# Transposed keys copied once into a compact buffer and placed in the padded operand by two DMAs, with the scores issued behind the next query projection

## The reference, cut to what matters

```python
        qkv = x @ Wqkv
        q, k, v = jnp.split(qkv, 3, -1)
        q = l2norm(q) * qs
        k = l2norm(k) * ksc
        q = q * cos * scale + rotate_half(q) * sin * scale
        k = k * cos * inv + rotate_half(k) * sin * inv
        ...
            sim = jnp.einsum('bhwie,bhwje->bhwij', bq, bk2) * QK_SCALE
            attn = jax.nn.softmax(sim, -1)
            out = jnp.einsum('bhwij,bhwje->bhwie', attn, bv2)
        ...
        return out @ Wo
```

## Time and profile before

| | us |
|---|---|
| median of 3 runs | 3313.89 |
| lowest, highest | 3313.37, 3315.62 |
| profiled execution, its own time | 3315.39 |
| span of the profiled execution | 3313.5 |

### The profile page before, as it was taken

One profiled execution on the slowest core, in us unless ns is written; L12 is line 12 of the kernel. 1 busy time (PEld: TensorE's weight loads), 2 busy tenths in 40 slices (PEclk: granted clock), 3 DMA queues, 4 the chain that ended last, 5 costly groups with the idle time before them and its releaser, 6 DMA issues. The chain is left out here.

```text
span 3313.5 us, 78774 instructions
## 1 busy us (share of the span) xinstructions
PE 3069.6 (93%) x28844; PEld 2169.1 (65%) x28844; DVE 2496.2 (75%) x3265; ACT 2434.9 (73%) x3708; POOL 2060.2 (62%) x1410
## 2 busy tenths in 40 slices
PE   8288886899999999999999999999999999999996
PEld 6276675666666676666666666666666666666662
DVE  3788886777778777787777777777777777777772
ACT  3366664687877787878787787878787877787872
POOL 0356554766666666666667666667666666666660
PEclk9689897999999999999999999999999999999997
DMA  1000001100001100001000011000110000100002
GB/s 45 13 23 22 19 22 45 37 20 19 19 19 26 45 19 19 19 19 53 19 19 19 16 26 45 19 19 19 27 45 19 19 19 17 32 21 19 20 19 58
DMA packets 80509, 84.53 MB, mean 26 GB/s; under 512 B 23734, under 2 KB 53908, under 8 KB 79668
## 3 DMA queue, kind: packets, MB, share of 16 engines
q1 hardware_dynamic: 79988, 82.40, 9.3%
q0 software_dynamic: 448, 1.20, 0.1%
HBM read 22.72 MB, written 2.10 MB: 7 GB/s over the span
## 5 line engine op out<-in xcount | busy, mean ns | idle before, releaser
L1325 POOL TENSOR_TENSOR qk_r<-qk_r,qk_t 128x1024 f32<-128x1024 f32 x384 | 915.6, 2385 | 669.0 <-DVE qk_r L1181 438.8
L807 PE MATMUL pa<-w_hi,xs_hi 128*128 128x512 f32 x1152 | 583.6, 507 | 68.6 <-DVE w_lo L1261 38.4
L1174 DVE TENSOR_REDUCE ss<-sq 128x16 f32<-128x1024 f32 x384 | 464.0, 1208 | 63.1 <-ACT sq L983 63.1
L1036 ACT COPY kT<-px 64x1024 f32<-64x1024 f32 x384 | 385.0, 1003 | 119.2 <-PE px L835 114.5
L1181 DVE TENSOR_TENSOR qk_r<-pa,rot 128x1024 f32<-128x1024 f32 x384 | 465.9, 1213 | 0.0
L1190 DVE TENSOR_TENSOR qk_t<-pa,rot 128x1024 f32<-128x1024 f32 x384 | 465.7, 1213 | 0.0
L807 PE MATMUL pa<-w_hi,xs_lo 128*128 128x512 f32 x1152 | 458.1, 398 | 0.0
L807 PE MATMUL pa<-w_lo,xs_hi 128*128 128x512 f32 x1152 | 457.4, 397 | 0.0
L835 PEld LDWEIGHTS px<-ident_sb,qk_r 128*128 128x128 f32 x3072 | 361.4, 142 | 113.3 <-issue 74.9
L1334 POOL TENSOR_TENSOR qk_r<-qk_r,inv 128x1024 f32<-128x1024 f32 x192 | 370.6, 1930 | 57.0 <-ACT inv L1020 55.1
L835 PE MATMUL px<-ident_sb,qk_r 128*128 128x128 f32 x3072 | 401.1, 274 | 4.5 <-POOL qk_r L1334 4.5
(11 more groups left out here) (156 smaller groups left out, 5315.9 us busy)
## 6 DMA issues: line engine op xcount, KB each, us to landing
pT<-prT SPq DMA_DIRECT2D x768, 64.0 KB, 2.0
w_raw<-in_Wqkv SPq DMA_DIRECT2D x6, 1536.0 KB, 6.7
s_x_turn<-c_xn SPq DMA_DIRECT2D x32, 128.0 KB, 2.0
s_x<-c_xn SPq DMA_DIRECT2D x32, 128.0 KB, 1.9
wo<-in_Wo SPq DMA_DIRECT2D x6, 512.0 KB, 4.1
c_x_ring<-in_x SPq DMA_DIRECT2D x32, 64.0 KB, 1.8
o_x<-in_x SPq DMA_DIRECT2D x8, 256.0 KB, 4.6
out<-o_out SPq DMA_DIRECT2D x8, 256.0 KB, 4.2
```

The source lines that it names most:

```text
L807: last = pe.matmul(pa[(u + c) % 2][:, half * 512:half * 512 + 512], x[:, j * P:(j + 1) * P], w[:, at], start=(k == 0), stop=(k == 2))
L1036: act.copy(kT[rows, :, :, half, :].rearrange("p h b j -> p (h b) j"), px[rows, :].rearrange("p (h j) -> p h j", j=S)).then_inc(s["tk_out"], 1)
L1174: dve.reduce_sum(ss[:, c, :], heads(sq[:]), AX.X).then_inc(s[sum_sem], 1)
L1325: pool.tensor_tensor(qk_r[:, j % 2, c, :], qk_r[:, j % 2, c, :], qk_t[:, c, :], ALU.add)\
```

## The change

The transposed keys go in one instruction of 128 partitions from `px` into a new compact buffer `k_both`. Two DMAs on SyncE's queue then place the upper and lower 64 partitions in `kT`, whose layout is changed so that each DMA writes one contiguous row of 1024 elements per partition. A new semaphore, `kT_loaded`, tells TensorE that they have landed. The matmuls of `scores` read their 64 columns as two pieces of 32. `tk_out` counts one per tile, not two. In slots 1 to 3, `scores` is called after `project_q` and not before it; in slot 0 the order is as it was.

```diff
-        kT = sb("kT", [P, HP, TILE_B, 2, S])
+        k_both = sb("k_both", [P, HP, P])
+        kT = sb("kT", [P, 2, HP, TILE_B, S])
...
+                        n, _, live = tile(i, j, 1)
+                        if live:
+                            sp.wait_ge(s["tk_out"], n + 1)
+                            wait_for(sp, s["scores_done"], n)
+                            for half in range(2):
+                                rows = slice(half * DH, (half + 1) * DH)
+                                sp.dma_start(kT[rows, half].rearrange("p h b j -> p (h b j)"),
+                                             k_both[rows].rearrange("p h n -> p (h n)")).then_inc(s["kT_loaded"], 16)
...
-                        pe.wait_ge(s["tk_out"], 2 * (n + 1))
+                        pe.wait_ge(s["kT_loaded"], 32 * (n + 1))
...
-                                                 kT[:, hp, b, :, :].rearrange("p h j -> p (h j)"), start=False,
-                                                 stop=True, skip_group_check=True)
+                                                 kT[:, :, hp, b, :], start=False, stop=True, skip_group_check=True)
...
-                            pe.wait_ge(s["tk_out"], 2 * (n + 3))
+                            pe.wait_ge(s["tk_out"], n + 3)
...
                     for j in range(GT):
-                        scores(i, j)
+                        if j == 0:
+                            scores(i, j)
                         project_q(i, j)
+                        if j > 0:
+                            scores(i, j)
...
-                        for half in range(2):
-                            rows = slice(half * DH, (half + 1) * DH)
-                            act.copy(kT[rows, :, :, half, :].rearrange("p h b j -> p (h b) j"),
-                                     px[rows, :].rearrange("p (h j) -> p h j", j=S)).then_inc(s["tk_out"], 1)
+                        wait_for(act, s["kT_loaded"], 32 * n)
+                        act.copy(k_both[:].rearrange("p h n -> p (h n)"), px[:]).then_inc(s["tk_out"], 1)
```

More of the change, by code:

```diff
@@ L679, in stack @@
             sq_q sq_k sum_q sum_k floored ln_done inv_ready
-            cos_q cos_k sin_q sin_k rot_q rot_k norm_k tq_done tq_out tk_done tk_out v_out
+            cos_q cos_k sin_q sin_k rot_q rot_k norm_k tq_done tq_out tk_done tk_out kT_loaded v_out
             scores_done top_done sub_done scaled exp_done den_done rden_done probs_done turned pT_loaded pv_done pv_out
```

## The result

The changed kernel takes 3328.17 us as the median of 6 runs (3327.59 to 3332.33), against 3313.91 us (3313.37 to 3316.60, 6 runs) before. The ratio is 1.0043, with a 95% interval of 1.0030 to 1.0056: it is slower by 14.3 us. The profiled one of before took 3315.39, 1.5 us more than its median. So differences of the two traces overstate the change by up to 2.7 us. Of all the executions timed here only one ran at a much lower granted clock (0.595): it took 4805.22 us, belongs to the version with the early mask and an early a-block, and the median of that version's other five is 3295.09 us.

What follows compares the result with a forecast made beforehand. TensorE was taken as the bound, idle 0.28 of a 54.77 us group. Profiled: 3315.39 + 5 (weight loads) + 1 (`sin_k`) - 1 (weighting) = 3320.4; median forecast 3313.89 + 5 = 3319, range 3306 to 3340.

Steps and rivals of the forecast that it cites:

- the 0.28 us wait: TensorE's one recurring wait, line 1181, for the queries' cosine product in slot 1; claimed to stay, 45 times, 12.4 us in all.
- Rival 2: ScalarE's saved microsecond reaches TensorE, returning 14.7 us of bare weight loads; slot 0 shorter by 0.3 us; 3304 us, chance 0.12.
- 4.0 us for the pair: Landing of a tile's two key DMAs after the first issue: 0.6 plus 2.9, plus 0.5 for both in flight together.
- my 0.7: Slot 0 without the swap: scores at 1511.80 against keys at 1512.5, so 0.7 us short.
- Rival 1: Keys land late and TensorE waits in slot 1 for `kT_loaded`: 48 x 0.5 = 24 us, so 3343; chance 0.17.
- The loss per group: Swap leaves weight loads bare on TensorE: +0.08, +0.00, +0.05 us in slots 1, 2, 3; +6 us in all, taken as +5.
- `sin_k` and the later maximum: Earlier `project_q` needs `sin_k`, about even, 0 to 0.1 us a group; maximum about 1.5 us later, absorbed by idle time.
- The key DMAs ahead of the weight loads: On SyncE's queue, thirteen loads start about 4 us later, five times in the run; costed at nothing.
- Rival 3: Swap costs more than weight loads: `sin_k` race lost by 0.2 to 0.3 us a group, or slower scores; 3330, chance 0.16.

## Why the prediction came out as it did

I forecast 3319 us and gave "slower" 0.42 and "same" 0.45. It became 3328, slower by 14.3 us where the sum had 5, within the range of 3306 to 3340. The steps:

- **The bound was read rightly.** TensorE is full in the steady groups, the 0.28 us wait stayed at 45 times, and ScalarE's 194 us bought nothing. Rival 2 fell: slot 0 is 0.03 us shorter, not 0.3, and it is so with the swap alone too, whose copies are the old ones.
- **The key DMAs were sized rightly and covered.** I took 4.0 us for the pair; it is 0.58 for the first issue and 3.7 of the second one's landing, 4.3. The swap covers that, as worked out, and nothing else does: undone, the slot is 1.02 us longer, where 4.3 in place of 4.0 makes my 0.7 into 1.0. Rival 1 fell in the steady groups and holds for one place, the end of the run. (Its price of 24 us counts the semaphore's 0.1 us once more than the sum above it; without that it is about 20.) The Trainium skill, "DMA: Bandwidth & Descriptors", section on rules for kernel authors, has two halves of the partitions serialize on the same engines. The trace agrees: of the pair issued from 1517.34 on, the core's 16 DMA engines are busy for 98% of 1518.5 to 1520.5 us, so the two halves do share them. No run here placed the keys in one DMA, so whether the rule's remedy helps was not tried. The page's fit, which it gives for DMAs that GpSimd issues, makes 3.2 us (an estimate) of this pair, 1.1 us less than the 4.3 measured.
- **The loss per group was sized nearly right, and in part by luck.** Forecast +0.08, 0.00 and +0.05 us in slots 1 to 3, and measured +0.10, +0.005 and +0.06: 7.5 us in 46 groups instead of the 5 that I took (6 by its sum); 6.4 of them stand in the swap alone. The single steps differ from my working. Behind the weighting, a projection matmul loses 0.1 us and the mask nothing that can be seen (its step is 0.32 us there and behind a projection alike). Behind the scores, the gate block loses 0.12 and a projection 0.10. I had charged each load in full (190, 179 and 96 ns) behind short matmuls and nothing elsewhere. The mask's 96 show nowhere. And the projection's 0.1 us isn't tied to short matmuls: it is 0.33 us behind the weighting and behind the scores, but also 0.31 behind the variance matmul (1508.02 to 1508.33 in the trace of before). It stands in both orders and cancels. What is left is the gate block's 0.12 and, in slot 3, L835's 0.06. So the places were right and the sum near, but the rule that gave it, a load bare at its full length, is not what the traces show.
- **`sin_k` and the later maximum** cost nothing that the steady groups show, as forecast (0 to 0.1 us a group). The key DMAs ahead of the weight loads, costed at nothing, show once: at 1573.71 the weighting waits 0.26 us for its `pT` DMAs, which stand behind the thirteen loads.
- **The term that was mis-sized is the one that I did not write: the first group and the end.** The sum ran over 48 equal groups. The timed swap alone gives +11.5, of which 6.4 are steady; the DMAs add 3. That leaves about 7 of the 14.3 us outside the steady groups. The traces put them at the start (the scores stand behind a projection that waits for data, and VectorE waits 4.64 us for them), at the end (the keys late by 2.3 us, +1.7), and 0.2 to 0.4 us in each of two groups behind which weights are loaded. How much each holds stays open: the swap in the first group alone costs 0.7 to 6.6 us by its median and 1.3 in its trace, 4.2 to 4.3 in the two traces whose first scores met the lower clock, and with the first group in the old order the median regains nothing (there the scores wait for the keys instead).
- **Rival 3** (3330) has the nearest time, but not its causes: the scores take 1.03 us as before (1522.13 to 1523.16), and no race for `sin_k` is lost in the steady part.

## What to carry to other kernels

Before an engine is relieved, look who waits for it: 194 us less work on ScalarE were worth nothing, because TensorE was full in every steady slot but for 0.28 us. A wait that is covered by moving a step costs what that step pays at its new neighbours, in every pass, and again in the first and the last pass, where the engine isn't full and the cover isn't there; these two belong in the sum as terms of their own. Before a difference of two traces in such a pass is put down to the change, compare them ahead of the first place where the order differs, and with a third trace. And on a full TensorE the order of the small steps is worth more than the work of other engines: moving one 0.3 us matmul to where a wait or a stream hides it gave 27 us (0.8%), the fastest version here, at 3286.4 us.

## What was not expected of the hardware

Ahead of a narrower part of the array (the 128\*64 and 128\*32 in the rows) about 0.1 us of TensorE's time is lost. A projection matmul of 512 columns takes 0.23 us in its stream and as the last one ahead of a matmul of the same width (1514.09 to 1514.33 in the trace of before: 0.24), but 0.33 as the last one ahead of the weighting (1509.25 to 1509.58) and 0.31 as the last ahead of the scores. As the first behind the weighting (1520.32 to 1520.65 after) or behind the scores it takes 0.33 too, but that is hardly a matter of width, for it takes 0.31 behind the variance matmul, which is as wide as the projection (before):

```profile
1507.17 1.02 PE L907 MATMUL pg<-fsq,mean_sb 128*128 128x512 f32 x2
1508.02 0.47 PE L807 MATMUL pa<-w_hi,xs_hi 128*128 128x512 f32 x1
1508.33 0.40 PE L807 MATMUL pa<-w_lo,xs_hi 128*128 128x512 f32 x1
```

The gate block does lose by standing behind the scores: 0.97 us against 0.85. The mask, 128 wide between 64 and 32 wide, added 0.32 us there and 0.15 in a stream of its own width. And the weighting is no longer ahead of the scores (1.89 us) than ahead of the mask (1.90), so there the step from 64 to 32 wide costs no more than the step from 64 to 128. The Trainium skill, "TensorEngine Tiling (Array Packing)", section on tiling modes, states that changing the mode drains TensorE; the rows ahead of a narrower part agree. What shows behind short matmuls may go with the length of the load as well, and no run here separated a drain from a load that isn't covered.
